# Last attention of a graph network: residual and second norm a turn earlier, the join inside the loop's last turns

## The reference

```python
q, k, v = [(x @ W + b).reshape(N, 8, 16) for W, b in ...]
e = (edge_attr @ We).reshape(-1, 8, 16)
alpha = einsum("ehd,ehd->eh", q[dst], k[src] + e) / 4
a = exp(alpha - segment_max(alpha, dst)[dst])
out = segment_sum(a / segment_sum(a, dst)[dst] * (v[src] + e), dst)
x_r = x @ Wskip + bskip
beta = sigmoid(concat(out, x_r, out - x_r) @ Wbeta)
out = beta * x_r + (1 - beta) * out
out = x + relu(layer_norm(out) * ln_gamma + ln_beta)
return layer_norm(x + out)          # the second norm
```

## Time and profile before

| | |
|---|---|
| median of 3 runs | 6258.33 us (6258.26, 6258.33, 6266.45) |
| profiled execution | span 6250.9 us; no time is listed for it beside its span |
| busy | DVE 5315.0 us (85%), ACT 4686.9 (75%), PE 4548.2 (73%), POOL 3804.5 (61%) |
| granted TensorE clock | 0.861 of full speed, mean over the span |
| the stage `angle` | from the first product at 5095.75 us to the end of the span |

### The profile page before, as it was taken

How to read it: one execution, slowest core, us unless ns; L and a number is a source line. 1 busy time by engine, 2 the same in 40 slices (tenths; PEclk the granted TensorE clock), 3 DMA queues, 4 the chain that set the end, 5 groups by cost and what they waited for, 6 DMA issues and landing times. The chain is left out here.

```text
span 6250.9 us, 117617 instructions
## 1 busy us (share of the span) xinstructions
PE 4548.2 (73%) x28601; PEld 3543.8 (57%) x28601; DVE 5315.0 (85%) x27201; ACT 4686.9 (75%) x14259; POOL 3804.5 (61%) x3880
## 2 busy tenths in 40 slices
PE   4143333333999979999979999949996769888881
PEld 2022222222888868888856777636654557666661
DVE  8767777774999978999969999957767859999996
ACT  7017888884999978999959999945545648888884
POOL 3057777763777737666366666447753445777774
PEclk9555555556999989999989999979998989999995
DMA  9377555553888845666547676646657954444441
GB/s 191 45 66 134 133 125 133 130 126 102 240 246 248 244 156 189 206 216 205 183 144 206 198 206 203 177 143 205 208 173 255 299 179 152 151 163 152 156 158 42
DMA packets 608007, 1075.90 MB, mean 172 GB/s; under 512 B 263700, under 2 KB 370015, under 8 KB 607193
## 3 DMA queue, kind: packets, MB, share of 16 engines
q1 hardware_dynamic: 476056, 787.63, 39.5%
q0 software_dynamic: 129920, 280.46, 20.6%
q10 hardware_dynamic: 1344, 0.30, 0.0%
HBM read 564.38 MB, written 530.59 MB: 175 GB/s over the span
## 5 line engine op out<-in xcount | busy, mean ns | idle before, releaser
L1925 POOL DMA_INDIRECT xs<-tab,rec x1176 | 1156.7, 984 | 358.4 <-issue 318.2
L2049 ACT ACTIVATE st<-xs,cb 128x128 f32<-128x128 f32 x2352 | 814.5, 401 | 0.9 <-DVE cg L1639 0.9
L2173 DVE SCALAR_TENSOR_TENSOR st<-st,cg 128x128 f32<-128x128 f32 x2352 | 719.5, 348 | 41.3 <-ACT st L2049 36.9
L1980 PE MATMUL p_y<-w_all,xt 128*128 128x258 f32 x2352 | 722.7, 390 | 30.6 <-DVE cA L2138 29.6
L2057 ACT ACTIVATE z<-p_a 128x384 f32<-128x384 f32 x1176 | 574.0, 488 | 119.3 <-PE p_a L1817 108.1
L1448 POOL DMA_INDIRECT in<-in_x,rec x392 | 388.0, 990 | 402.0 <-DMA rec<-meta 283.2
L2138 DVE CUSTOM_DVE_ANT_0 junk<-p_y,xs 128x129 f32<-128x129 f32 x2352 | 585.9, 288 | 11.4 <-PE p_y L1980 9.6
L1073 PE MATMUL p_m<-b_rows,ones_bf 3*128 3x512 bf16 x224 | 100.0, 446 | 648.3 <-ACT z L1116 648.3
L886 ACT ACTIVATE o<-y,norm 128x127 f32<-128x127 f32 (+1 forms) x1176 | 513.7, 488 | 6.8 <-DVE norm L880 6.7
L1817 PE MATMUL p_a<-ident,st 128*128 128x128 f32 x2352 | 468.1, 281 | 67.0 <-DVE st L2173 62.9
L2757 POOL DMA_INDIRECT xs<-res,rec x392 | 388.8, 992 | 198.8 <-issue 98.8
(11 more groups left out here) (778 smaller groups left out, 16334.5 us busy)
## 6 DMA issues: line engine op xcount, KB each, us to landing
states<-st SPq DMA_DIRECT2D x168, 910.0 KB
own<-tab SPq DMA_DIRECT2D x168, 448.0 KB
tab<-o SPq DMA_DIRECT2D x168, 448.0 KB
runs<-run SPq DMA_DIRECT2D x112, 448.0 KB, 6.8
tab<-out SPq DMA_DIRECT2D x112, 448.0 KB
x<-tab SPq DMA_DIRECT2D x112, 448.0 KB
xd<-tab SPq DMA_DIRECT2D x168, 192.0 KB, 3.5
angles<-st SPq DMA_DIRECT2D x56, 532.0 KB
```

Of the source, the lines that this page charges most:

```text
L1925: pool.indirect_dma_start(xs[:, i, j, 0:D], None, table, bass.IndirectOffsetOnAxis(ap=rec[:, i, SRC, j : j + 1], axis=0)).then_inc(got_in[ ...
L1980: ins = pe.matmul(p_y[two(c, i)][:, 0 : H * X1], xt[:, four(c, i), 0:D], k.w_qk[:], start=True, stop=True)
L2049: ins = act.activation(state_of(r, j)[:, h, :], xs[:, c.slot(UB), j, 0:D], ACT.Copy, scale=co.b[:, c.slot(2), h, j : j + 1])
L2173: ins = dve.scalar_tensor_tensor(mine[:, h, :], prev[:, h, :], co.g[:, c.slot(2), h, j : j + 1], mine[:, h, :], ALU.mult, ALU.add)
```

## The change

1. The lags of the residual and of the second norm are one turn less. DVE's `affine` and statistics are for chunk u-3 and stand in columns 3, 4, 5 and 6 (before: 1, 3, 4 and 5 for chunk u-4); the aggregates `second.sums` stand at the very end of the turn, behind `mix` (before: in column 6). Log, root and application are for chunk u-4, POOL's scatter for chunk u-5, SP's node numbers for chunk u-3. The drain has 4 turns on ACT and DVE, 5 on POOL and 3 on SP, each one less.
2. The join moves into the last turns of the same block. `merge_parts` becomes the class `Join` with a method for each piece. With turn 55 the last full turn: POOL gathers `mine` in turn 55 and `kept_row` in turn 56, DVE has the maxima (`tops`) at the end of turn 56, the weights at the end of 57, the totals at the end of 58. The join's second transposes use `p_t[0]` in place of `beside`. PE's part follows its loop.
3. `RowNorm` is replaced by `RowPieceNorm` for that row: ACT's Ln and Exp and a Newton step on DVE in place of POOL's power. The same class `Join` serves the three earlier layers with the same instructions in the same place.

```diff
-    def root(self, pool):
-        pool.wait_ge(self.asked, 1)
-        pool.tensor_tensor(self.mv[:, 1:2], self.mv[:, 1:2], self.k.root[:], ALU.pow).then_inc(self.rooted, 1)
...
+class RowPieceNorm:
...
+    def log(self, act):
+        y = self.s[:, 0:1]
+        act.wait_ge(self.asked, 1)
+        act.activation(y, self.mv[:, 1:2], ACT.Ln, bias=self.lift, scale=PieceNorm.LN_SCALE).then_inc(self.logged, 1)
+        act.wait_ge(self.logged, 1)
+        act.activation(y, y, ACT.Exp, scale=-0.5).then_inc(self.guessed, 1)
...
+        def is_at(t, u, i):
+            return t == k.TN - 1 and u == UB - 1 + i
...
             @b.gpsimd
...
+                    if is_at(t, u, 0):
+                        pool.wait_ge(turned, k.NB * J)
...
+                        pool.indirect_dma_start(mine[:], None, table, join_row, bounds_check=k.NR - 1, oob_is_err=False).then_inc(mine_in, 16)
+                    if is_at(t, u, 1):
+                        for i_ in range(UB):
+                            pool.wait_ge(kept[i_], k.TN * 16)
+                        pool.indirect_dma_start(kept_row[:], None, k.angles, join_row, bounds_check=k.NR - 1, oob_is_err=False).then_inc(fetched, 16)
...
-                    done = Chunk(k, t, u, -6)
+                    done = Chunk(k, t, u, -5)
...
             @b.scalar
...
-                        if j == 0 and c5.there:
-                            second.log(act, c5)
+                        if j == 0 and c4.there:
+                            second.log(act, c4)
...
+                    if is_at(t, u, TOPS):
+                        join.exponentials(act)
+                    if is_at(t, u, WEIGHTS):
+                        join.untangle(act)
+
+                walk(k, act, one, SCORE + 1, 4, 1)
...
             @b.vector
...
-                        if c5.there and j in (2, 3):
-                            second.root((j - 2) * 3, dve, order, c5)
+                        if c4.there and j in (2, 3):
+                            second.root((j - 2) * 3, dve, order, c4)
...
-                        if c4.there and j in (1, 3, 4):
-                            affine({1: 0, 3: 1, 4: 2}[j], c4)
+                        if c3.there and j in (3, 4, 5):
+                            affine(j - 3, c3)
                         if c2.there and j == 0:
                             first.sums(dve, order, c2)
-                        if c4.there:
-                            if j == 5:
-                                dve.wait_ge(resid, c4.count(1, 1))
-                                second.stats(dve, order, e[:, c4.slot(RING)])
-                            if j == 6:
-                                second.sums(dve, order, c4)
+                        if c3.there and j == 6:
+                            dve.wait_ge(resid, c3.count(1, 1))
+                            second.stats(dve, order, e[:, c3.slot(RING)])
                     if c2.there:
                         first.root(3, dve, order, c2)
                     if mid.there:
                         spread(mid)
                     if c1.there:
                         mix(c1)
-
-                walk(k, dve, one, SCORE, 5, 1)
+                    if c3.there:
+                        second.sums(dve, order, c3)
+                    if is_at(t, u, TOPS):
+                        dve.wait_ge(fetched, 16)
+                        join.tops(dve, step)
+                    if is_at(t, u, WEIGHTS):
+                        join.weights(dve, step)
+                    if is_at(t, u, TOTALS):
+                        join.totals(dve, step)
...
+                step = Chain(dve, join_done)
+                walk(k, dve, one, SCORE, 4, 1)
```

More of the change, by code:

```diff
@@ L22 @@
 EAHEAD = 5
+TAIL = 1
 JN = 7
@@ L1662 @@
     EXP, ASKS = 3, 2
[L1665 to L1681, removed]
-            for h in range(n):
[L1683 to L1692, removed]
-            for h in range(g * n, (g + 1) * n):
[L1694 to L1710, removed]
@@ L1716, in vector, with weights @@
-            dve.nop().then_inc(exp_in, 1)
-        for g in groups:
-            dve.wait_ge(exped, g + 1)
+            step(dve.tensor_tensor(part(mine, g), part(self.head_m, g), part(top, g), ALU.subtract))
+            dve.nop().then_inc(self.exp_in, 1)
+    def weights(self, dve, step):
+        k, part, side, over, each = self.k, self.part, self.side, self.over, self.each
+        e, w, sum_, inv, was = self.e, self.w, self.sum, self.inv, self.was
+        for g in self.groups:
+            dve.wait_ge(self.exped, g + 1)
@@ L2017, in _ @@
                 pe.wait_ge(scored, k.NB * J)
-                merge[0](pe)
+                join.rows(pe)
+                join.turns(pe)
+                join.sums(pe)
                 pe.wait_ge(fetched, 48)
@@ L2803, in _ @@
                 walk(k, pe, one, SCORE + 1, 0, 1)
+                pe.wait_ge(scored, k.NB * J)
+                pe.wait_ge(v_out, k.NB * J)
+                pe.wait_ge(mine_in, 16)
+                pe.transpose(p_q[2][:, 0:D], mine[:], k.ident[:]).then_inc(f_turned, 1)
+                pe.matmul(p_o[1][:, 0 : D + 1], k.ones_bf[:], b_own[:], start=True, stop=False)
+                pe.wait_ge(f_copied, 1)
+                pe.matmul(p_o[1][:, 0 : D + 1], mt[:], w_own[:], start=False, stop=True).then_inc(f_made, 1)
+                pe.wait_ge(state_done, k.NB)
+                join.rows(pe)
+                pe.wait_ge(f_zf, 1)
+                join.turns(pe)
+                join.sums(pe)
             @b.scalar
@@ L3004, in one @@
                             logit(1, c1)
-                        if c5.there and j == 2:
-                            second.root(1, dve, order, c5)
+                        if c4.there and j == 2:
+                            second.root(1, dve, order, c4)
                         if c1.there and j == 4:
@@ L3014, in one @@
                             logit(2, c1)
-                        if c5.there and j == 2:
-                            second.root(2, dve, order, c5)
+                        if c4.there and j == 2:
+                            second.root(2, dve, order, c4)
                         if c1.there and j == 4:
```

232 lines of the change are left out of this document (140 added, 92 removed).

## The result

The kernel after takes 6505.6 us (median of 4 runs, 6503.85 to 6508.7) against 6260.17 of the kernel before beside it (4 runs, 6258.26 to 6266.45): a ratio of 1.0384 [1.0371, 1.0396], slower. The direction and both mechanisms of the forecast were right, the time was 65 us above it and 31 above the range.

A forecast was written before the change was run, and what follows sets the result against it. The prediction took DVE to bound the loop at 18.4 us a turn, POOL just behind; 6250.9 − 30 (drain) + 115 (ring) + 100 (clock) = 6435.9, with 7.4 to the median 6443, put at 6441 us, range 6333 to 6475.

The forecast's parts named there:

- both mechanisms of the forecast: Loop: ACT waiting for late aggregates lengthens each turn, 115 us; PE's clock halves in the resulting gap, 100 us.
- the ring: Loop: ACT's log waits for DVE's turn-end aggregates, DVE for ACT's copies; 20.8 us a turn against 18.4, 115 us more.
- the clock: Loop, PE idle ahead of column 2: half rate at nearly every gap, 2.0 us a turn, 100 us more.
- the drain: After the loop: the join's work moves among the last turns' norms and scatters; 30 us less, bounds 24 to 36.
- The late log: ACT's second-norm log, column 0: waits for aggregates now at DVE's turn end, 3.5 to 5 us each turn.
- the waits for cfa and the gate: ACT's idle time ahead of the scores' exponential (1.53 us) and of y (0.46); claimed to vanish when ACT is late.
- 50 turns: Loop turns 4 to 53, having both late log and products; each was to lose 2.3 us, before any clock loss.
- the walk: One pass round the loop's waits: ACT's log to last copy 13.5 us, DVE's part 7.2, hand-overs about 0.1; 20.8 us.
- the 0.60 ahead of column 4: ACT's wait for PE ahead of column 4's copies, 0.60 us, claimed to stay when ACT is late.
- the rival without it (6343): Loop: late aggregates stop ACT but PE stays at 2.4 GHz or falls now and then; 6343 to 6400 us, chance 0.24.
- five of six gaps of 2.02 us: Batch norm's stage, PE's gaps: read as leaving the clock alone five times in six, evidence for the full clock staying.
- The joined row's norm: Drain: estimated at some 6.6 us on DVE and ACT, claimed to run under the last scatters.

The follow-up runs named there:

- the run with PE filled: Kernel after plus nine unused matmuls on PE ahead of column 2's products, against the kernel after: 6400.77 us, a turn of 21.55.

## Why the prediction was off, step by step

Two terms of the sum were too small: the ring (115 us, measured 152) and the clock (100 us, measured 117). The cause, the direction and the drain held.

- **The late log: right, shown.** Undoing this one place gives 258 us back; doing it alone costs 202 (6459.78 against 6257.5). ACT's wait was forecast at 3.5 to 5 us and is 4.4; the waits for cfa and the gate went, as told.
- **50 turns: right.** 269.4 us over 5.38 is 50.1.
- **The ring, "20.8 us": mis-sized, it is 21.55.** The DVE part was 7.2 and measured 7.3 (5713.18, the end of the last column's copy, to 5720.47). The ACT part was put at 13.5 and is 14.26 (5698.92 to 5713.18). I had left one wait for PE in the walk, the 0.60 ahead of column 4. In the run with PE filled there are two, 0.24 ahead of column 3 and 1.09 ahead of column 4, 0.73 more. Once ACT is late, PE starts column 2 with ACT's copy and needs its 2.30 us for each further column, while ACT would be ready sooner; in the earlier trace rows PE had a head start that hid this. The walk took an idle time of before as a constant, though the change moved the engine that it waits for. The term is 50 × 3.04 = 152 us in place of 115.
- Of these 3.04, 1.21 come from the statistics behind the last product: from the end of the last column's copy to the next log it is 7.29 us here and 6.08 with the statistics in column 5 (5723.40 to 5729.48). I had taken 1.4. The other 1.83 are the aggregates' place (20.34 against 18.51); I had left about 1.0 for them. Most of the difference is the walk's missing 0.73.
- **The clock, "2.0": mis-sized, it is 2.34.** That it falls in every turn was right; the rival without it (6343) falls by the granted clock of 0.86 and by the run with PE filled. Column 2's product to column 3's takes 4.31 in place of 2.30 us, the 2.0 that I had. But the low rate lasts into column 3's product too: from there to column 4's it takes 2.62 (5720.72 to 5723.34), 0.3 more. The term is 117 us in place of 100. The rule of "TensorE: Matmul & The Clock Gate" in the Trainium skill ("HAM oscillation — how this bites in real kernels"), that each iteration starts at the half rate, agrees with the trace: 1.25 against 0.71 us behind the gap.
- The weight of that rival rested on a misreading. I wrote that five of six gaps of 2.02 us left the clock alone. Three of the five gaps between the two slow pairs of the earlier trace rows are shorter:

```profile
4800.88 1.12 PE L2562 MATMUL p_y<-x,ident 128*128 128x512 f32 x2 [1.67 <-ACT o L945]
...
4806.64 1.12 PE L2562 MATMUL p_y<-x,ident 128*128 128x512 f32 x2 [1.67 <-ACT o L945]
...
4812.43 1.13 PE L2562 MATMUL p_y<-x,ident 128*128 128x512 f32 x2 [1.69 <-ACT o L945]
```

Over that whole stage 9 of the 16 pairs behind a gap of 1.98 to 2.03 us ran slow, not one in six.

- **The drain, "30 us less": right.** 29.3 less from the last `spread`. The first scatter of chunk 54 stands 45.2 us behind turn 56's first instruction (forecast about 45), and the 14 and the joined row's scatter go at 1.27 each, as the timelines of DVE and POOL show:

```profile
6437.11 0.21 DVE L3033 TENSOR_REDUCE gate<-st 128x7 f32<-128x56 f32 x1
```

```profile
6482.26 0.97 POOL L2849 DMA_INDIRECT out<-o,nodes  x1 [9.56 <-ACT o L887]
...
6500.16 1.00 POOL L2854 DMA_INDIRECT out<-xs,head_out  x1 [0.31 <-issue]
```

- With both terms as measured the sum is 6250.9 − 30 + 152 + 117 = 6490, and 12.5 of the stages ahead make 6502, against a span of 6503.8. Of the 65 us that the forecast was short, 37 are the ring's term and 17 the clock's; 5 are the stages ahead (12.5 against the 7.4 added for the median). The joined row's norm ran under the last scatters.
- Open: why the clock's price is 2.11 on average, and changes from turn to turn, in one order of DVE's work and 2.34 in every turn of the other; the gaps differ (3.5 and 4.7), but no run changed the gap alone. The 2.11 also rests on the estimate of 20.34: no run with fewer matmuls in the gap measured it.

## What to carry to other kernels

A small instruction that another engine waits for belongs ahead of long work that nobody waits for: 0.56 us of aggregates, issued 4.5 us after they could be, cost 5.0 us a turn (23.89 against 18.85), since everything queued behind the waiting log slipped too. Right behind its inputs was good, a few other instructions later was best (18.47). Where it can't move, let the engine that waits do other work first: the log one column later took the turn to 19.58. When you walk such a ring, walk it with every engine at its own pace from the point of release; one wait of 0.60 us read before the change became two, 0.24 and 1.09. When you fill an engine's gap to find what the gap costs, make the filling shorter than the gap: 4.17 us in a gap of 3.5 held the ring up and hid a part of the clock's price. And part a change before judging it: here a drain worth 29 us was buried under a loop that cost 269, and it could be had alone.

## What the runs showed of the hardware

- In this loop PE's clock fell within a gap of 4.7 us in each turn of 23.9 (granted 1.00 from 5713 to 5714 us, 0.50 from 5715 to 5721.4) and stayed at its 1.2 GHz level up to about 5721.4, although PE worked from 5716.41 on. Nine matmuls, 4.17 us of PE's time and without any use for the result, held it at 2.4 GHz and took 100 us off the loop.
- With the log behind column 1's copies PE had a gap of 1.65 to 1.70 us in each turn, and the granted clock was 0.91 or 0.92 in twelve turns and 1.00 in seven: the same order of work cost 20.1 us in some turns and 18.7 in others.
- Busy time hides short waits. DVE was listed as busy for 496.79 of 500 us in a loop in which two of its instructions a turn started 0.12 us late for ACT's copies, because the record of the instruction ahead reaches past the point where the next could start.
- The stages ahead of the last one, identical instructions, ended up to 12.5 us apart from one profiled execution to the next.
